# Two of eight feed-forward chunks of fourteen items rectified by ScalarE and GpSimd, with the five engines' orders written anew

## What is computed

```python
xn = layernorm(x)
for i in range(6):
    n1 = layernorm(s, ln1)                       # s starts as xn
    q, k, v = n1 @ wq[i], n1 @ wk[i], n1 @ wv[i]
    q = softmax(q, over a head's 16 features);  k = softmax(k, over the tokens)
    s = (q @ (k.T @ v)) @ wo[i] + bo[i] + s      # eight heads
    h = layernorm(s, ln2) @ w1[i]                # 128 -> 512
    h = where(h >= 0, h, 0.01 * h)
    s = h @ w2[i] + s
y = (xn @ expert_w[top1] + expert_b[top1]) * top_probability
out = x + s * silu(y)
```

## Time and profile before

| | us |
|---|---|
| median of 3 runs | 596.42 |
| lowest, highest | 594.59, 596.98 |
| the profiled execution's own time | 596.75 |
| its span in the trace | 594.9 |

### The profile page before, as it was taken

The page is one execution under the profiler, slowest core; times in us unless marked ns, Lnnn a source line. Parts: engine busy times, 40 slices in busy tenths (PEclk is TensorE's granted clock), DMA queues, the critical chain, the costliest instruction groups (busy, mean ns, idle before and its releaser), DMA issues.

```text
span 594.9 us, 12614 instructions
## 1 busy us (share of the span) xinstructions
PE 578.7 (97%) x4166; PEld 516.3 (87%) x4166; DVE 540.1 (91%) x1352; ACT 434.8 (73%) x763; POOL 311.1 (52%) x308
## 2 busy tenths in 40 slices
PE   7999999999999999999999999999999999999897
PEld 7899897887978889889889898898898898898796
DVE  6887999999988999999999999999999999988865
ACT  2658595876976868868768768768779678687652
POOL 5896134755852772442442532433523766867752
PEclk9989999999999999999999999999999999999999
DMA  8209233323224154445435435445342351441102
GB/s 282 75 10 328 72 110 121 124 94 130 95 84 152 71 152 146 112 133 169 124 123 163 109 141 150 116 163 158 103 165 80 108 167 57 129 156 62 45 36 106
DMA packets 74946, 73.20 MB, mean 123 GB/s; under 512 B 27265, under 2 KB 65153, under 8 KB 74882
## 3 DMA queue, kind: packets, MB, share of 16 engines
q1 hardware_dynamic: 72400, 68.18, 35.6%
q0 software_dynamic: 2048, 4.20, 2.3%
q10 hardware_dynamic: 434, 0.02, 0.0%
HBM read 39.87 MB, written 32.51 MB: 122 GB/s over the span
## 4 chain that ended last, share of the span: by engine, by line
PE 75%; DVE 11%; DMA 4%; issue 3%; POOL 3%; ACT 2%; SPq 1%; DVEq 0%; ACTq 0%; POOLq 0%
PE psY L513 23%; PE psH L406 6%; PE psS L558 6%; PE psH L407 6%; PE psH L408 6%; PE psT L592 6%; PE psT L401 6%; PE psT L526 5%; PE psM L538 5%; DVE st L1295 2%; PE psS L455 2%; DMA through<-blocks 1%; DVE X L1563 1%; DVE hid L1553 1%; DMA turned<-through 1%
## 5 line engine op out<-in xcount | busy, mean ns | idle before, releaser
L513 PE MATMUL psY<-w_all,hid 128*128 128x128 f32 x1536 | 188.7, 276 | 2.5 <-DVE hid L1553 1.8
L513 PEld LDWEIGHTS psY<-w_all,hid 128*128 128x128 f32 x1536 | 182.0, 193 | 6.6 <-issue 2.3
L1553 DVE TENSOR_TENSOR hid<-psH,hsl 128x512 f32<-128x512 f32 x192 | 127.2, 676 | 13.6 <-ACT hsl L936 13.1
L936 ACT ACTIVATE hsl<-psH 128x512 f32<-128x512 f32 x192 | 108.3, 591 | 42.0 <-PE psH L408 38.5
L2038 POOL TENSOR_TENSOR rstd<-veps,minus_half 128x8 f32<-128x8 f32 x44 | 72.7, 1653 | 61.2 <-DVE veps L1312 61.0
L2134 POOL TENSOR_TENSOR qsm<-qe,qrec 128x1024 f32<-128x1024 f32 x24 | 46.5, 1938 | 97.8 <-DVE qrec L1636 97.8
L2112 POOL TENSOR_TENSOR xn_lo<-xn,xn_hi 128x512 fp32r<-128x512 f32 x48 | 60.6, 1282 | 69.4 <-ACT xn_hi L1000 69.4
L406 PE MATMUL psH<-xn_hi,w_hi 128*128 128x512 f32 x192 | 86.4, 450 | 3.7 <-DVE hid L1553 3.4
L966 ACT ACTIVATE xh<-X,shift,rstd 128x128 f32<-128x128 f32 x188 | 77.0, 482 | 8.9 <-POOL shift L2041 8.7
L408 PE MATMUL psH<-xn_lo,w_hi 128*128 128x512 f32 x192 | 76.1, 396 | 0.0
L407 PE MATMUL psH<-xn_hi,w_lo 128*128 128x512 f32 x192 | 76.0, 396 | 0.0
(11 more groups left out here) (161 smaller groups left out, 1024.9 us busy)
## 6 DMA issues: line engine op xcount, KB each, us to landing
through<-turn SPq DMA_DIRECT2D x22, 512.0 KB, 2.7
turn<-through SPq DMA_DIRECT2D x88, 128.0 KB
through<-blocks SPq DMA_DIRECT2D x20, 512.0 KB, 3.2
turned<-through SPq DMA_DIRECT2D x80, 128.0 KB, 2.8
wb<-expert_rows SPq DMA_DIRECT2D x40, 128.0 KB, 2.0
sorted_x<-blocks SPq DMA_DIRECT2D x5, 512.0 KB, 4.4
...
```

Source lines behind the costliest of these rows:

```text
L513: last = nc.tensor.matmul(tile(psY, t), tile(hid[:, c, :], t), w2_all[:, n // NBATCH, c, :], start=(c == 0 and t == 0), stop=(c == NC - 1) ...
L936: nc.scalar.activation(hsl[:, i % 2, :], psH[:, i % 2, :], ACT.Copy, scale=SLOPE) \
L1553: nc.vector.tensor_tensor(hid[:, i % NC, :], psH[:, i % 2, :], hsl[:, i % 2, :], ALU.max) \
```

## The change

**The pooled chunks.** For items 7 to 20 the chunks 2 and 5 are rectified without VectorE, as max(h, 0.01 h) = 0.01 h + relu(0.99 h): after `slope` has written hsl, ScalarE makes a second pass over the same bank of psH, Relu with scale 0.99, into hid (counted in `h_copied`), and GpSimd adds hsl to hid in place (`hid_pooled`). VectorE skips these 28 chunks. The bank of psH is free once the second pass has read it; hsl is free once GpSimd has added it; `output` waits for `hid_pooled`.

**The orders.** All five lists are written in another order, in the first ten slots, in `slot` and behind it, and so is SyncE's order of the first loads (w1[0] goes behind the inputs, w2[0] and the experts' weights ahead of the attention weights of layers 1 to 5). The computation and its instructions are otherwise the same. The core of the diff:

```diff
@@ helpers
+        POOLED = (2, 5,)
+        POOLED_FIRST, POOLED_END = 7, 21
+
+        def pooled(n, i):
+            return POOLED_FIRST <= n < POOLED_END and i in POOLED
+
+        def pooled_before(n, i):
+            whole = max(0, min(n, POOLED_END) - POOLED_FIRST)
+            return whole * len(POOLED) + sum(1 for c in range(max(i, 0)) if pooled(n, c))
...
@@ TensorE, hidden and output
-                    wait(pe, "hid_ready", NF * n + i - 1)
+                    if pooled(*two_before(n, i)):
+                        pe.wait_ge(sig("h_copied"), pooled_before(*two_before(n, i)) + 1)
+                    else:
+                        wait(pe, "hid_ready", by_vector_before(*two_before(n, i)) + 1)
...
-                    pe.wait_ge(sig("hid_ready"), NF * n + i + 1)
+                    if pooled(n, i):
+                        pe.wait_ge(sig("hid_pooled"), pooled_before(n, i) + 1)
+                    else:
+                        pe.wait_ge(sig("hid_ready"), by_vector_before(n, i) + 1)
...
@@ ScalarE, slope
-                        wait(act, "hid_ready", NF * n + i - 1)
+                        if pooled(*two_before(n, i)):
+                            act.wait_ge(sig("hid_pooled"), pooled_before(*two_before(n, i)) + 1)
+                        else:
+                            wait(act, "hid_ready", by_vector_before(*two_before(n, i)) + 1)
                         nc.scalar.activation(hsl[:, i % 2, :], psH[:, i % 2, :], ACT.Copy, scale=SLOPE) \
                             .then_inc(sig("hsl_ready"), 1)
+                        if pooled(n, i):
+                            act.wait_ge(sig("y_done"), NF * n + i - 3)
+                            nc.scalar.activation(hid[:, i % NC, :], psH[:, i % 2, :], ACT.Relu, scale=1.0 - SLOPE) \
+                                .then_inc(sig("h_copied"), 1)
...
@@ VectorE, leaky
+                        if pooled(n, i):
+                            continue
...
@@ GpSimd
+            def leaky(n, i):
+
+                if pooled(n, i):
+                    pool.wait_ge(sig("h_copied"), pooled_before(n, i) + 1)
+                    nc.gpsimd.tensor_tensor(hid[:, i % NC, :], hid[:, i % NC, :], hsl[:, i % 2, :], ALU.add) \
+                        .then_inc(sig("hid_pooled"), 1)
...
@@ TensorE, slot(s)
                 key_sums(s - 1)
+                hidden(s - 3, 4)
                 output(s - 3, 2)
+                hidden(s - 3, 5)
                 context(s - 1)
-                hidden(s - 3, 4)
-                hidden(s - 3, 5)
+                hidden(s - 3, 6)
                 mixing(s - 1)
+                queries_by_feature(s - 1)
                 output(s - 3, 3)
-                queries_by_feature(s - 1)
-                hidden(s - 3, 6)
                 hidden(s - 3, 7)
...
@@ VectorE, slot(s)
                 leaky(s - 3, 0)
+                leaky(s - 3, 1)
+                key_maxima(s - 1)
                 variances1(s)
-                key_maxima(s - 1)
-                leaky(s - 3, 1)
                 query_maxima(s - 1)
...
@@ GpSimd, slot(s)
                 move_rows(s, 0)
-                move_rows(s, 1)
                 if s % NBATCH == 3 and s < ITEMS:
                     split_w1(s // NBATCH)
                 low_part(s - 3, 0)
+                move_rows(s, 1)
+                deviations2(s - 2)
                 low_part(s - 3, 1)
-                deviations2(s - 2)
                 move_rows(s, 2)
+                deviations1(s)
+                leaky(s - 3, 2)
                 move_rows(s, 3)
-                deviations1(s)
                 scale_queries(s - 1)
+                leaky(s - 3, 5)
```

548 lines of the change are left out of this document (276 added, 272 removed).

## The result

| | before | after |
|---|---|---|
| median (4 runs each) | 596.38 us | 608.59 us |
| lowest, highest | 594.59, 596.98 | 606.33, 612.54 |
| profiled execution, its span | 596.75, 594.9 | 606.92, 605.2 |

The ratio is 1.0217, 95% interval 1.0153 to 1.0281: the change makes the kernel 2.2% slower. The forecast was 597.5, range 590 to 604.

The account below looks back on a forecast made before the run. TensorE was taken to bound the kernel; 596.75 + 0 (pooled chunks) + 1.3 (gathers) + 0.6 (tail) + 0 (slots 0 to 9) = 598.65, or 598.3 against the median. It said 597.5, range 590 to 604.

Parts of the forecast that it names:

- The pooled chunks in the full stretch: From 225 to 465 us TensorE is always busy and covers VectorE's relief, so pooling gains 0; the main term.
- rival 2: Slots 10 to 23: path from hidden chunk 4 to next keys outgrows TensorE's cover; slower, 605 us, chance 0.10.
- the gather term: Slots 21 to 23: GpSimd's additions beside gathers cost 2.7 us, vanished xnT waits return 1.4; net +1.3, bounds -1.4 and +4.
- The tail: Behind slot 23: silu(0) moved ahead makes a new 2.9 us TensorE wait, partly offset; net +0.6, bounds -1.1 and +2.
- the wait at 563.88: TensorE's 1.76 us wait near the end, forecast to go with weigh(3) moved, as would 1.7 us of half clock.
- Slots 0 to 9: Reordered slots without pooled chunks, before 225 us: two places priced, rest not; taken as 0, bounds -5 and +5.
- the first stage ends as before: Start of the kernel: no change, since query_sums(0) still stands behind four input statistics.
- The clock: In the tail, the new idle time may drop the clock to 1.2 GHz again; 1.7 us added.
- the 10.6 us: TensorE's idle and slow-clock time outside the start and last output; the most any new order could recover there.
- rival 3: Early stretch loses 3 us more, plus GpSimd's gather slots or port clashes with VectorE; about 602 us, chance 0.21.

Follow-up runs that it names:

- e9: Kernel after with the kernel before's lists ahead of slot 10 and behind slot 23, leaving pooling and new slot order; 599.55 us, ratio 1.0000.
- e16: As e9 but without the pooling, so only the new order of slots 10 to 23 on the kernel before; 596.43 us, ratio 1.0005.
- e5: The kernel after, unchanged, measured again as the base of the second round; 609.69 us, ratio 1.0239 to the kernel before.
- e6: Kernel after with VectorE's cast of the first w1 moved behind finish_mix(0) and the input half behind it; 606.06 us, ratio 1.0159.
- e15: Kernel after with useless TensorE transposes, 12 in front of logits(1) and 22 in front of keys_by_token(23); 604.13 us, ratio 1.0157.
- e11: Kernel before with GpSimd's last gathers ahead of weigh(2) and weigh(3) right behind it; 604.33 us, ratio 1.0077.
- e17: Kernel before with 14 useless TensorE transposes in front of hidden(22,2); ratio 0.9997.
- e18: Kernel before with GpSimd's weigh(3) behind deviations2(23) and add_input(0,1) behind the last low parts; ratio 0.9994.
- e1: Kernel before with its own lists and only the 28 pooled chunks added; 603.46 us, ratio 1.0101.
- e4: Kernel after with the kernel before's lists behind slot 23 on all engines; 605.03 us, ratio 1.0160.
- e8: Kernel after with silu(0) and its table load moved behind keys_by_token(23) on ScalarE; 605.22 us, ratio 1.0149.
- e3: Kernel after with the kernel before's lists ahead of slot 10 on all engines, first loads included; 601.59 us, ratio 1.0076.
- e10: Kernel after with the moves of e6 and e8, attention(6) ahead of hidden(5,1), and attention_input(8) behind queries_by_feature(7); 606.26 us, ratio 1.0112.
- e14: As e13, plus attention(6) moved two hidden chunks ahead of keys(7) and VectorE's add_attention(6) ahead of leaky(5,1); 603.38 us, ratio 1.0129.
- e7: Kernel after with the kernel before's order of the first loads on SyncE and ScalarE; 609.78 us, ratio 1.0225.
- e13: Kernel after with the two moves of e6 and e8 together; 601.56 us, ratio 1.0117.
- e2: Kernel after with its new orders on all five engines but no chunk pooled; 607.39 us, ratio 1.0152.

## Why the prediction was wrong, step by step

**The pooled chunks in the full stretch, 0: right.** 28 second passes at 0.585 us and 28 additions at 1.276 us came within 1% of the rows taken for them, VectorE's busy time fell to 218.84 us (216 forecast), a slot kept its 22.96 us, and e9 and e16 measure 1.0000 and 1.0005. The additions met none of VectorE's eight-number operations there: between 225 and 465 us none of those took over 0.3 us in after, where before had ten of 0.6 to 0.8 us beside its subtractions. This was called the main term, and it was; but a main term of zero decides nothing.

**The path from hidden chunk 4 to the next keys (rival 2): right in size, without spare.** Forecast were 11.95 us of path under 12.88 us of cover. After's trace has the same path with 9.1 instead of 8.5 us through HBM. ScalarE in slot 12, from the slope of chunk 4 to xnT, and TensorE's keys behind it:

```profile
258.14 0.60 ACT L964 ACTIVATE hsl<-psH 128x512 f32<-128x512 f32 x1
...
269.44 1.25 ACT L1014 ACTIVATE xnT<-turned,lnp 128x1024 f32<-128x1024 f32 x1 [3.29 <-DMA turned<-through]
```

```profile
270.79 1.94 PE L551 MATMUL psT<-xnT,wk_all 128*128 128x512 f32 x4
```

That is 12.6 us from the slope to the end of xnT, and keys begin as it ends. The missing spare shows in single waits, which differ from execution to execution: between 225 and 472 us TensorE waits for xnT for 0.8 us in two places in after, 1.8 in three in e5, 2.1 in three in e6, 1.4 in four in e9, and not at all in e15 or in before. In the median of e9's 12 runs they don't show. Here are those of slots 15 and 23:

```profile
340.14 1.98 PE L551 MATMUL psT<-xnT,wk_all 128*128 128x512 f32 x4 [0.34 <-ACT xnT L1014]
```

```profile
523.79 1.98 PE L551 MATMUL psT<-xnT,wk_all 128*128 128x512 f32 x4 [1.25 <-ACT xnT L1014]
```

The second says that a step of the gather term was wrong: the wait for xnT in slot 23, 1.00 us at 516.77, did not go, it grew. The term was +1.3 and the trace has +0.9 against before, so its size was right by luck; against e11, e17 and e18 it would be -1.1. What the term missed is e1: in the old order the same additions cost 3.5 to 5.5 us there. With the new slot order they don't, and VectorE's eight-number sum takes 0.17 us in slots 21 to 23 of after. That fits the new place of deviations1, ahead of the last gathers, but no run moved this step alone.

**The tail, +0.6: a failed size.** Measured by removal: 4.7 us (e4, more without its slowest run), or 4.5 by the silu alone (e8). The new wait was forecast as 2.9 us and is 2.51, at 557.00. Three things were missed. The transposes behind it can run at half clock, 1.97 us in after's trace, where they take 1.09 at full clock (e5). I took back the wait at 563.88 as gone, and it is, but weigh(3), moved behind the last gathers, now meets the last half norm. VectorE, GpSimd and TensorE of the kernel after, and VectorE and GpSimd of e8:

```profile
577.44 2.78 DVE L1390 TENSOR_SCALAR xh<-X,rstd,shift 128x128 f32<-128x128 f32 x4
...
578.00 1.89 POOL L2129 TENSOR_TENSOR gate<-gate,top_weight 128x1024 f32<-128x1024 f32 x1 [1.57 <-DMA gate<-sorted_y,row_index]
...
580.33 1.07 PE L420 MATMUL psM<-ident,xh 128*128 128x128 f32 x8 [1.86 <-issue]
```

```profile
577.46 1.11 DVE L1390 TENSOR_SCALAR xh<-X,rstd,shift 128x128 f32<-128x128 f32 x4
...
578.77 1.89 POOL L2129 TENSOR_TENSOR gate<-gate,top_weight 128x1024 f32<-128x1024 f32 x1 [1.55 <-DMA gate<-sorted_y,row_index]
```

TensorE waits 1.86 us there in after. In e8 the weighing comes 0.2 us behind the four multiplications instead of between them; they take 1.11 instead of 2.78 us, and TensorE doesn't wait. So the gain of e8 holds this wait too: the new wait and this one are 2.5 + 1.9 = 4.4 us, and 4.5 were measured, with no clock regained. That the weighing came late enough in e8 was not arranged; e15 still has this wait, 1.77 us at 577. The Trainium skill ("SBUF — State Buffer", Who interferes with whom) says that VectorE's multiplications by a scalar can take the port pair that GpSimd uses, and that the one which issues first has it; both rows agree. And a gain of 3.5 us was booked for the wait at 563.88 with its half clock. In before itself e17 and e18 remove that cost from the trace and move the median by less than 1 us, in e18 with a new wait of 1.15 us in its place.

**Slots 0 to 9, 0 with bounds of ±5: the step that failed.** They cost 6 us in the trace and 9.7 us by e3, outside the bounds. The two places that were priced went the way they were priced: first_row takes 0.16 instead of 1.26 us, and attention(7) waits for qsmT behind xnT, 0.62 us where 1.2 were said. The error was to let two priced places and an even bound stand for five lists rewritten over 190 us. One sentence of it was plainly wrong, that the first stage ends as before: the cast of w1, put beside GpSimd's qsm, makes the mix of item 0 late, and e6 gets 3.6 us back by moving that one step, 1.4 of them the wait and about 2.5 clock. A second, keys(7) close behind attention(6) with their shared bank, was in the order to be read and was not read; e10 and e14 show that its wait of 1.4 us is not to be had by moving those steps, only changed for another. Of the 9.7 us, 3.6 are settled by one move. The rest, most of it between 90 and 180 us of work, stays open: e7 excludes a gain from the order of the first loads, and with the two repairs that do work e13 is still 1.2% slower than before.

**The clock: charged once, due several times.** I counted 1.7 us for one stretch at 1.2 GHz. The traced execution of before had a second one, from 35.6 to 39.0 us, so the 10.6 us called the most that could be recovered were 1.7 too few. In after the waits of 1.4 and 2.5 us, those that e6 and e8 remove, are each followed by 3.4 us at half clock, 1.7 us lost, and the runs of e5 put about 4 of 14.5 us on the clock. In other executions of the same places the clock stayed up: at 557 us it fell in after, e2 and e6 and not in e3, e5 and e7. e15 shows that the wait need not cost clock: with 34 useless transposes in those two waits the useful work waits as long as before, and about half of the 5 us that it gains is clock. In e15 the transposes of expk, behind 22 fillers:

```profile
552.64 2.56 PE L893 MATMUL psS<-ident 128*128 128x128 f32 x22
555.31 1.09 PE L420 MATMUL psT<-ident,expk 128*128 128x128 f32 x8
```

The transposes take 1.09 instead of 1.97 us. Since a fall follows a wait in some executions only, and single falls stand where no wait is, what a wait costs by the clock is an average.

**Chances.** Slower had 0.31. Nearest came rival 3, about 602 by 3 us more in the early stretch: the right place, half of the size in the trace and a third by e3. What should have widened the range is that its largest bounds stood on a stretch without a working.
